# A fifth stream on TensorE: matmuls of zeros into an open sum, with the steps of all engines in a new order

## The reference, cut to what matters

```
h = tok(x)                       # Reformer-like block: hashed attention, two gelu MLPs
h = h + mamba_both(norm(h))      # two selective scans over time, forward and backward, 16 states x 256 channels,
                                 # then an MLP of width 512 with two layer norms
h = h + experts(norm(h))         # 8 experts, top 2 by softmax; out += comb[:, e] * (gelu(x @ w1[e] + b1[e]) @ w2[e] + b2[e])
h = h + attention(norm(h))       # 8 heads whose mask leaves sums over later positions
h = h + nibble_logic(h)          # small MLPs with relu, rounding and one-hot digits
```

## Time and profile before

| | us |
|---|---|
| median of 3 runs | 3890.96 |
| lowest, highest | 3883.97, 3895.62 |
| profiled execution | 3896.18 |
| its span, first to last instruction | 3893.9 |
| VectorE busy in it | 3420.1 |
| TensorE busy | 3127.3 |
| ScalarE busy | 2925.3 |
| mean granted clock | 0.887 |

### The profile page before, as it was taken

The page is one execution under the profiler, slowest core; times in us unless marked ns, Lnnn a source line. Parts: engine busy times, 40 slices in busy tenths (PEclk is TensorE's granted clock), DMA queues, the critical chain, the costliest instruction groups (busy, mean ns, idle before and its releaser), DMA issues.

```text
span 3893.9 us, 31221 instructions
## 1 busy us (share of the span) xinstructions
PE 3127.3 (80%) x8728; PEld 1368.3 (35%) x8728; DVE 3420.1 (88%) x4654; ACT 2925.3 (75%) x3806; POOL 1337.2 (34%) x644
## 2 busy tenths in 40 slices
PE   5655878889787788979888888979788887877797
PEld 3231423334343333424343333424343333432232
DVE  1499979999898999999999999999999998999822
ACT  2546887987868888787888878787888879686442
POOL 0254333333323334343433443343433433333200
PEclk8757788989888899989999999989989999888797
DMA  1233333424324243333434342343424333333310
GB/s 63 77 108 96 113 109 92 128 80 135 99 94 118 93 131 95 119 118 109 125 98 123 107 131 94 121 117 109 124 95 126 104 116 104 104 119 104 100 49 11
DMA packets 209022, 404.60 MB, mean 104 GB/s; under 512 B 25936, under 2 KB 34256, under 8 KB 208592
## 3 DMA queue, kind: packets, MB, share of 16 engines
q1 hardware_dynamic: 206800, 398.41, 32.8%
q0 software_dynamic: 2048, 4.20, 1.0%
HBM read 387.57 MB, written 14.94 MB: 103 GB/s over the span
## 4 chain that ended last, share of the span: by engine, by line
PE 37%; DVE 26%; ACT 25%; issue 12%; POOL 0%; DMA 0%; DVEq 0%; ACTq 0%; POOLq 0%
PE bank_a L569 8%; DVE states L921 7%; PE bank_b L580 7%; ACT L705 6%; DVE states L927 6%; ACT decay L705 6%; DVE y_sum L932 3%; ACT L701 3%; ACT tok L705 3%; ACT last L705 3%; ACT middle L705 3%; PE bank_p L478 1%; PE bank_c L397 1%; PE bank_p L421 1%; PE bank_c L640 1%
## 5 line engine op out<-in xcount | busy, mean ns | idle before, releaser
L1199 POOL TENSOR_TENSOR dbu<-dtu,b_rows 128x1024 f32<-128x1024 f32 x512 | 1243.4, 2431 | 2104.1 <-DVE states L921 1823.6
L921 DVE TENSOR_TENSOR_SCAN states<-decay,dbu 128x512 f32<-128x512 f32 x1024 | 1298.7, 1311 | 38.1 <-ACT decay L705 30.5
L705 ACT ACTIVATE decay<-dt,neg_a 128x508 f32<-128x508 f32 x1024 | 659.4, 707 | 64.6 <-DVE states L921 59.0
L705 ACT ACT_TABLE_LOAD x516 | 662.0, 1283 | 47.5 <-PEq L344 16.6
L569 PE MATMUL bank_a<-middle,experts 128*128 128x512 f32 x1024 | 616.2, 687 | 97.1 <-ACT middle L705 88.9
L705 ACT ACTIVATE middle<-bank_a,columns 128x512 f32<-128x512 f32 x608 | 417.8, 687 | 329.6 <-PE bank_a L569 305.4
L927 DVE TENSOR_TENSOR states<-states,c_rows 128x512 f32<-128x512 f32 x960 | 610.8, 679 | 0.3
L932 DVE TENSOR_TENSOR y_sum<-y_sum,states 128x512 f32<-128x512 f32 x960 | 609.9, 674 | 0.2
L580 PE MATMUL bank_b<-middle,experts 128*128 128x512 f32 x1024 | 572.7, 643 | 21.4 <-ACT middle L705 11.8
L705 ACT ACTIVATE last<-bank_c 128x512 f32<-128x512 f32 (+2 forms) x320 | 201.0, 634 | 198.0 <-PE bank_c L617 52.4
L701 ACT ACT_TABLE_LOAD x232 | 297.7, 1283 | 46.0 <-PE bank_p L469 17.0
(11 more groups left out here) (206 smaller groups left out, 3944.7 us busy)
## 6 DMA issues: line engine op xcount, KB each, us to landing
b_rows<-bc_scratch SPq DMA_DIRECT2D x512, 256.0 KB, 3.4
c_rows<-bc_scratch SPq DMA_DIRECT2D x512, 256.0 KB, 3.3
experts<-ew SPq DMA_DIRECT2D x128, 512.0 KB, 3.5
comb_rows<-comb_scratch SPq DMA_DIRECT2D x128, 256.0 KB, 3.8
h_scratch<-tok SPq DMA_DIRECT2D x16, 256.0 KB, 3.3
x_scratch<-xin SPq DMA_DIRECT2D x16, 256.0 KB, 3.8
xr<-x_scratch SPq DMA_DIRECT2D x16, 256.0 KB, 4.9
h<-h_scratch SPq DMA_DIRECT2D x16, 256.0 KB, 5.3
```

The lines of the kernel that those rows point to most:

```text
L705: return nc.scalar.activation(out, in_, func, **more)
L921: tick(nc.vector.tensor_tensor_scan(hs[:, h, ::step], da[:, n % DECAYS, h, ::step], dbu[:, n % AHEAD, h, ::step], 0.0, ALU.mult, ALU.add), ...
L1199: tick(nc.gpsimd.tensor_tensor(dbu[:, n % AHEAD], dtu[:, k % 2], row, ALU.mult), "a_dbu")
```

## The change

1. A tile `zeros` of 128x128 bfloat16 is set to 0 on DVE, ahead of DVE's first wait in the set-up block.
2. TensorE gets a stream **F**, `nothing_added`. Each step is one matmul of the zeros with 512 columns of a bfloat16 table (`selections`, four times the same 128 columns), added to bank B with `start=False, stop=False`: it adds 0. It waits for nothing and signals nothing. It has 1435 steps, in 328 runs of 1 to 30, all at places where a sum in bank B is open: 905 in the experts, 530 in the MLP ahead of them.
3. `neg_a`, the scale of the Exps that make `decay`, is no tile of its own any more but is made in place in `weights`.
4. The strings of all five engines are new. Letters of P, C, D and A are as many as before on every engine. Nothing repeats itself any more.

```diff
-    NEGA = sb("neg_a", [128, 2 * HALVES * DS])
+    ZERO = sb("zeros", [128, 128], BF16)
     EW = sb("experts", [128, 2, 2 * FF])
+
+    NEGA = W[:, AT["falog"][0]:AT["falog"][0] + 2 * HALVES * DS]
...
         def _(dve):
+            nc.vector.memset(ZERO[:, :], 0.0)
             dve.wait_ge(done["b"], len(FOLD))
...
-            drive("PE", P=each(token), C=whole(fold, middle), D=beside())
+            def nothing_added():
+                finite = sel("fieldcum").rearrange("p (a t) -> p a t", a=1).to_broadcast([128, SEQS, 128])
+                for _ in range("".join(ORDER["PE"]).count("F")):
+                    mm(seqs(B), ZERO[:, :], finite, start=False, stop=False)
+                    yield
+
+            drive("PE", P=each(token), C=whole(fold, middle), D=beside(), F=nothing_added())
...
-        "PPPPPPPPPPPDDPDDDDDDPPPCDCDPPCDPPCCDPPCCPCCCPCPCPCPPPCCCCCCCPCCPPCCPPCCPPCCPPCCPPCCPPCCPPCCPCCCCPCPC"
...
+        "PPPPPPPPPPPDDDPDDPDPPDDPPPPPPPPPPPCPCPDDCFFFFFFFFFFFFFFFFFFFCCPFDCCDCCPPFFFFFPPFFFFPPFFFFFCCPCPCPPPC"
```

More of the change, by code:

```diff
@@ new lines @@
+        "PPCPCCPCFFFFFCCPCCPCCPCCPCCFFFFFFFFPFFFFFFCCFCCPPCCFCCPPFCCFFFFFFFFFFFFFCCPPCCFCCPFFFCCPFFFFFPFFFFFF"
+        "FFFFFDCCDDPCCDFFCCFFDCCFFFFDFFPFFFFFFFFFPFFFFFFFFFFFFCCDCCPCCDCCPPFFFFFFFFFFFCCPPCCFCCPPFCCFCCPCCPFF"
+        "FPFFFFFFFFFFFFFPCCDDPPFFCCPCCCCPCDCCPPDFCCFFFFFFFFFPPFFFFPPFCCFCDDPCDPCPPCDPPDCPPCDPDDPDCCCPCCPCCPCC"
+        "DCCDFFFPDFFFDDCCFPPDCCDCCPPDCCDDFFFFFFFFFFFFFCCPPFCCDCCPDDCCPDDPFFFCCDCCFFDCCPCDCCCDCCFFFFFFFFFFDFFF"
+        "FFFDCCDCCDCCDCCDCCDPPCCDCCDDPFCCDCCDDPCCDPCCFFDCCFPDPCCCPCPPDDCPFFFFPFFFCCDDFFCCFFDCCFFFFDFPFFFFFFFF"
@@ new lines @@
+        "FPFPFFPFFFFFFFFFDDFFFFFFDFFFFFFCPCPPDDPPCPPCDPDDPDCPPCDPPDDPPCCCPDCCPCCPCCPCCPCCDFFFFFDPDFFFDDCCDFFF"
+        "FFFFFCCPPCCDCCPPDCCDDFFFFDCCPPDCCDCCPDCCPCCDPPDCCCCDCCFCCDCCDDFFDDFFFFFFFFCCDCCDCCDCDCCCDPFFFCCPDDFF"
+        "CCDCCFFFFDFFFPFFFFFFFFFFFFCCPPFCCDCPPDCPPPPCPDCDPCFPPFFFCCPFDCCFFDFFFFFFFFFFFFFFFFFFFFFFFFFFFFFFDDFC"
+        "CPCDCPPCPCPDPPDCDPCDPDDDDCCCPPDCCDDPPDFFPPDFCCDCCPDDPCCPCCDCCPCCPCCDCCDDFFPFFFFFCCDCCPPDCCDCCPCCPDFF"
+        "FFDFFFCCPPCCFFFFFFFFFFFDFFCCPDCCPCPCCDDCFFFFFDDDPFFFCCPCCPCCDCDDCPFDDCCDDFFCCFFDFCCPDPCCFFFFFFFFFFFF"
@@ new lines @@
+        "FCCPPDCCDPCPDCCPDCPPCPCCDPPDFCCPFFFFFFFFFFFFFFFFFFFFFFFFFFDDFFFFDFPCCFFFFPPDDCDCDPPDPCPDCPDDPCPPCPPD"
+        "CCPCPDDFCCDCCPDFFPCCPCDPCCCPDDFFFFFFFCCDCCPCDCCCPPDCCDDFFFFFCCDPPCCDCCPPCCDCCPDPCCFFPDFFFFFFFDPDDFCC"
+        "DCCDCCDCCFCCFCCDDDFFFFFFCCDCCDDPCCDPFCCFFDCCDPCCPCCPCCPPCDDCPPCPDCPDPCFFFFFFFFPCCDPPDFFCCPFFFFFFFFFF"
+        "FFFFFFFFFFFFFFFFDDFFFDFPFCCFFFFPPDDCDCDPPDPCPDCPDDPCPPCPPDCCDDCPPDFCCDCCPDDPDFFFCCPCCPCCPCCDCCDDPDDC"
+        "CPPDCCDCCPPCCDCCPPDCCFFFFFFFFFFFFFFFDFFCCDPFCCPCPDCCCDDDPDFFFFFCCFCCPCDDCCCDCCPDDFFFFPFFFCCDDCCFFDCC"
@@ new lines @@
+        "FPDPCCFFFFFFFFFFFFFFFCCDPCPCCCPPCCDCPCCPCPCPDCCPPCCPCCDFFFFFFFFFFFFFFFFFFFFFFFFFCPDCPPDCPPCPPDDCPDCP"
+        "DDDCCPCPDCCDDPPDDFFPPDCCDDPFDFFPCCPCDPCCCPCCDDFDFFFFPFFFFDCCDPPCCDCCPPCCDCCPPCCDCCPDFCCPFFDPFDFCCDCC"
+        "PFFFFDFFFFCCDCCDCCDCCDCCDCCDFFPFFFPFFFCCDCDDCFFPDCCDDCCFDFFFCCDCCFPDPCCFFFFFFFFFFFFFFFCCDPCPDPPPPCCP"
+        "CPCPPFFFCCPDDFFCCFDFCCFFDFFFFFFFFFFFFFFFFFFFFFFFFFFDDFFFFDPFFCCPPDDPPCPPCDPDCPDCPPDDDCCCPPDCCDDPPDFF"
+        "PDFFCCPCCPCCPCCPCCDDFFFDPFFFFFFFFCCPPDCCDDPPDCCDFFFFCCDPPFCCDCCPDFFPDFPFFFFFFFFFFDFCCPCCDCCCDDCCCDDF"
@@ L75 @@
+        "CCCCFCCFCCFCCCCFCCFCCFCCCCFCCFCCFCDDDDDDDDDDDDDDDDDDDDDDDDDDDDDDDDDDDDD",
         "",
@@ L103 @@
+        "CDCDCCCDCDCDCCDCCCCDCCCCCCCCCCCCCCCCCCDDDDDDDDDDDDDDDDDDDDDDD",
         "",
@@ L167 @@
+        "AAPAAAPAACAAAAAACAACCCDAAADAAAACAAAACAAAAAAAADAAAAAAAAAAAAACACACAAAAAACAAAACAAAAAACAACAAAACCCAAAAAAC"
+        "AAAACADCCCCCDCCCD",
         "",
```

186 lines of the change are left out of this document (88 added, 98 removed).

## The result

The changed kernel takes 3906.3 us (median of 7 runs, 3901.3 to 3915.6), the kernel before 3891.0 on the same chip (7 runs, 3883.9 to 3900.9). The ratio is 1.0036, with a 95% interval of 1.0020 to 1.0051: slower by 15 us, a third of a per cent, where 3847 was forecast. The profiled execution took 3909.8 us, its span 3908.0, at a mean granted clock of 0.908 against 0.887.

A forecast was written before the change was run, and what follows sets the result against it. VectorE was taken to bound the middle, leaving only its idle time to win. Terms 10 - 10 - 47 + 0 + 3 = -44 us gave 3852 on the profiled execution, 3847 on the median; range 3785 to 3945.

The forecast's parts named there:

- the start: First 180 us: VectorE's 138 us of idle stay, as the first zero matmul comes behind the first scans.
- the tail: Experts' chunks behind the last scan: a zero matmul ends 0.09 us too late in each; 3 us slower taken.
- the spacing of the zeros: TensorE's zero matmuls: 0.22 to 0.23 us from start to start.
- their price in the queue: Awaited matmuls on TensorE stand behind runs of zeros: 0 to 62 us slower, 10 taken.
- the rival "by the order": Even middle groups lose their evenness, worth 61 us: 3952 us, or 3908 with the 44 us gain; chance 0.12.
- The rival in which TensorE falls behind: Zeros make each expert's sum half a run late: 62 us slower, 3953 us; chance 0.14.
- The rival in which zeros don't raise the clock: Clock stays about 0.89, zeros take up to 660 us of TensorE, which sets the time: 3913 to 4230 us; chance 0.03.
- The uneven order: Seven even middle groups stop repeating one order: 0 taken, up to 61 us slower kept for the range.
- The clock's worth: Earlier matmuls shorten VectorE's waits for experts' sums and other short waits: 0 to 40 us gained, 10 taken.
- a clock of 0.95 or more in the middle: Sign that the forecast is right: granted clock in the middle reaches at least 0.95, from 0.90 before.
- The table loads: ScalarE's loads fall from 748 to 670, 100 us less work; 0 to 93 us gained, 47 taken.
- the long waits: VectorE's few waits of up to 15.2 us in uneven stretches, some 93 us; about half was to go.

The follow-up runs named there:

- 2870: The changed kernel with each of its runs of zeros doubled in length: 3915.5 us, 1.0070 of the kernel before.
- spliced: Changed kernel with the old order, without zeros, in groups 6 to 13; changed order with zeros before and after: 3870.7 us, 0.9934 of the kernel before.

## Why the prediction was wrong

**Right.** 670 loads and ScalarE at 2824.0 (for 2825), the start, the tail (207.7 us behind the start of the last scan, 205.1 before: +2.6 for +3), the spacing of the zeros (0.22), and their price in the queue: 10 us were taken, and no net cost can be seen at 1435. (By the rates given the upper bound of that price is 64 us, not 62.) VectorE's busy time, 3419.9 for 3420, is right by luck: in the middle its instructions took 20 us more and in head and end 20 us less. The sign of the rival "by the order" came, 203 us of VectorE's idle time over 180:3600, in waits over all groups. The rival in which TensorE falls behind is out at 1435: its sign was L1129's wait well over 65.5 us, and it is 38.4. At 2870 it is 52.7, a cost but still not that sign. The rival in which zeros don't raise the clock is out.

**The step that failed: "The uneven order. I take 0".** It measures +65 us of VectorE idle in the middle and 20 us more by longer instructions; without the zeros the idle part is +105. The bound of 61 named beside it comes near the 65 in part by luck, since it knew nothing of what the zeros would take off. The reason given for the 0, that VectorE's sequence stays much the same "to within three" steps at each group's first scan, looks at counts at one point of the group. What made the waits that were followed is the distance in the queue between the start of a chain over other engines and the step that needs its end: 26 instructions in every old group, 2 where the wait is 9.7 us. The old repeated order has 3.3% of idle and no wait over 1.3 us in its seven even groups. The order put in its place idles like the uneven stretches before, which had 7.0%: the changed middle has 122 of 1836 us, 6.7%, and 163 of 1875, 8.7%, without its zeros.

**The second step that failed: "The clock's worth".** It was taken at 10 us, at most 40, from what VectorE waited for in the old order. For the old order that isn't far off: over 180:3600 21 of its 183 us of idle lie in low time, in the middle 3 of 57, and so the argument from the earlier trace rows, that VectorE is busy where the clock is low, holds there. It was carried over to an order in which it doesn't hold. In the new order without zeros 96 of 266 us of idle lie in low time, with them 48 of 203, and the zeros are worth some 65 us. A sign also failed: a clock of 0.95 or more in the middle was forecast, and over 180:3600 it is 0.92, with TensorE busy 2992 us for 2924, since the order alone had taken low time there from 713 to 961 us before the zeros brought it to 572. And the earlier trace rows don't bear out that the clock is low just where TensorE has little to do: it is 0.61 with 38 us of work and 0.77 with 33. The Trainium skill's advice to keep TensorE busy without gaps (TensorE: Matmul & The Clock Gate, section Why this matters for your kernels) would pay in both orders; the runs show it pays in one of them, and with 1560 zeros in the other, some of them behind a wait, it costs 0.3%.

**The table loads: right in size, given back elsewhere.** -47 was forecast for the long waits; head and end together lost 48 us of VectorE idle. But it isn't a gain of the loads alone. Without the zeros head and end lose only 15 us and nothing (73 and 192 us against 88 and 191), so two thirds of the 48 came with the zeros. How much of the head's 15 is the loads and how much the other moves of the same order wasn't separated.

**The sum.** Written with what was measured, against the profiled execution: start -3, head -32, middle +65, end -16, that is +14 on the span, from 3893.9 to 3908.0. The forecast had the outer terms in size and lacked the middle one. Two errors of opposite sign stood behind it: the order alone was 124 us worse than -44 (it is +80), and the zeros were some 65 us better than 0. That the miss is 59 us and not twice as much is their cancelling. The forecast had no term for VectorE's instructions that last longer, +20 in the middle.

**Left open.** In the kernels with the old middle behind the changed head its groups take 218 to 219 us and then 222 to 223, in one and the same order of letters (`spliced` 219, 219, 219, 218, 223, 222, 222), where the kernel before has 218 to 219 up to group 11 and then 220 and 222. So only part of it comes with the changed head; no run was made for that. Nor is it shown why the changed order has the lower clock at equal work (0.87 against 0.93 in the middle), or what the old order would gain by zeros in better places.

## What to carry to other kernels

Price a new order and the filler that comes with it apart, each on its own kernel, because the worth of the filler (here -13 or some 65 us) depends on the order that it fills and on its places in it. Before adding filler, see how much of the bounding engine's idle time lies in time at the low clock: 63 of 163 us in the new middle, 3 of 57 in the old one. Look too at what the filler stands behind: behind a wait it doesn't fill the pause but lengthens it. In a new order, count how much work of the waiting engine stands between the start of a chain and the step that needs its end. Compare stretch by stretch between events that both kernels have, idle time and busy time each for itself, since the same instructions can last longer, and keep the stretches that win: the changed head on the old middle is 0.9% faster than the kernel before and 1.2% with more zeros, where the whole change was 0.4% slower.
